# Linear attention's output side divided between both graph attentions (13 and 12 node tiles), and VectorE's copy of aggregated rows moved behind the next K copy

## The chip, the cores and the metric

The kernel runs on one core of a Trainium2 chip. Its time is the device time of one execution, in microseconds (us). The program writes instructions for five engines: TensorE (PE, with its weight loads shown as PEld), VectorE (DVE), ScalarE (ACT), GpSimd (POOL), and SyncE (SP), which mostly starts DMAs. Each engine works through its own queue in order; the queues meet only at semaphores.

## The reference, cut to what matters

There are 3125 nodes with 512 features and 53125 edges sorted by target. A layer of a mixed graph network is computed:

```
xn = layernorm(x)
# graph branch, two layers l = 0, 1
q, k, v = (xn @ Wq[l].T + bq[l]) / 8, xn @ Wk[l].T, xn @ Wv[l].T      # 8 heads of 64
w = softmax over the edges of one target of (q[dst] . k[src])
agg = segment_sum(w * v[src], dst);  attn = agg @ Wo[l].T + bo[l]
xn = batchnorm(xn + attn);  xn = batchnorm(xn + relu(xn @ W1.T + b1) @ W2.T + b2)
# mixing branch: linear attention on the first xn
q, k, v = softmax(xn Wq + bq), softmax(xn Wk + bk), xn Wv + bv         # softmax over a head's 64
mix = ((q @ (k.T v)) / (q . sum k) + q) @ Wp.T + bp
# then
x = x + layernorm(graph) + mix
out = x + mixture of 8 experts (top 2, 128 wide) on layernorm(x)
```

The change concerns the last line of the mixing branch, "mix", and the edge loop of the graph branch.

## The kernel before, in words

Stages follow one another: normalising and turning x; the Q, K and V products of layer 0 (stored in DRAM as Qd0 and KVd0); the mixing branch's products, which store the softmaxed q rows in DRAM (mixq) and leave the block matrix BD = k.T v in SBUF; the first graph attention; the joining of cut segments, the output product, batch norms and feed-forward of layer 0; the products of layer 1 (Qd1, KVd1); the second graph attention; the rest of layer 1; the experts.

**A graph attention** (`attend_pool`, `attend_pe`, `attend_dve`, `attend_act`) goes over 416 edge tiles of 128 edges. POOL gathers a tile's K and V rows with one indirect DMA (L1182, 128 rows of 4 KB) into a ring of 28 buffers. Eight tiles share one fetch of "slots", the rows of Q of the targets among them (L1191), and one indirect scatter of the aggregated rows (L1199). POOL may issue tile n once PE has turned tile n - 14, and once the buffer's former tile (n - 28) has been aggregated. The steps g = 0 to 105 each handle four tiles. In step g PE turns four K tiles (`turn_k`, L1270), runs the second half of an earlier group's aggregating matmuls after the second of them (`gather(..., 1)`, L1313), turns a one-hot tile for the slots in even steps (`turn_hot`, L1251) or the slots in odd ones (`turn_q`, L1262), turns the probabilities of group g - 2 (`turn_p`, L1277), adds masks (L1288), makes the scores (L1300), and runs the first half of the aggregation of group g - 2. Turned tiles go into PSUM banks that are used in a ring (`TURN_BANKS`: three banks in the first attention, five in the second). ACT copies three of four K tiles out of them (L1450) and makes the exponentials (L1469); DVE copies the fourth (`empty_k`, L1382), takes minima (L1375), normalises (L1389), copies turned probabilities (L1370), makes the one-hot tiles (L927), and copies the aggregated rows of eight tiles out of PSUM (`empty_agg`, L1395) for the scatter. `empty_agg` stands at the end of an odd step, ahead of the making of the one-hot tile.

**The mixing branch's output side** (`out_sp`, `out_pe`, `out_dve`, `out_act`) is written as generators that run in step with the first attention: every engine's loop calls `next(side)` at four places of a step. A node tile takes OUT = 16 such calls, so 25 tiles take 400 of the 424 calls. SP loads the tile's rows of mixq; PE turns them (L769, L770), multiplies with BD (L790, L792), turns the result again, and makes the product with Wp in twelve matmuls (L804 to L806: high and low parts of both factors); ACT and DVE copy and divide between; SP stores the rows to `mixd`, which the experts' stage reads. Wp is loaded once and cut into high and low parts during the first tile.

The second attention has no side work. Its K/V ring (`edge_views`) begins with buffers that are free early, and POOL issues nine gathers (`early`) before it waits for the stores of Q and for the end of the Q products. On SP's queue x is put away in DRAM (`put_x`, 6.25 MB) between the last K/V store and the first Q store of layer 1.

Of the kernel before, what the change touches and what calls it, by code (L numbers as in the profile page):

```python
# [6 lines left out]
P = 128  # L7
N, D, H, DH = 3125, 512, 8, 64
NT = 25
# [7 lines left out]
NJ = ET // NCH  # L17
# [65 lines left out]
def build(nc, A, out):  # L83
    with ExitStack() as ctx:
# [629 lines left out]
        TURN_BANKS, SC, AG = [[PS[4], PS[2], PS[3]], PS[0:5]], [PS[5], PS[6]], PS[7]  # L714
# [17 lines left out]
        OUT = 16  # L732
        WpH, WpL, WP_CUT = WoH, WA2r, 24
# [9 lines left out]
        def out_sp(views):  # L743
            qT, oT, qb, ob, outb, Wp = views
            sp.wait_ge(qkv_mm, QKV_E)
            sp.dma_start(Wp, kpo(A["MpT"])).then_inc(g_in, 16)
            sp.wait_ge(m_p, 3 * NT)
            sp.wait_ge(m_r, 3 * NT)
            sp.dma_start(rowsb[:, 1, :], A["mbp"].partition_broadcast(P)).then_inc(row_in, 16)
            for i in range(2):  # L750
                sp.wait_ge(mq_st[i], 16 * uses(NT, 2, i))
            fetch_q(0, qb)
            yield
            for s in range(OUT * NT):
                t, k = divmod(s, OUT)
                if k == 8 and t + 1 < NT:
                    fetch_q(t + 1, qb)
                if k == 15:
# [4 lines left out]
        def out_pe(views):  # L763
# [9 lines left out]
            pe.wait_ge(g_in, 16)  # L773
            pe.wait_ge(m_bd, 1)
            for s in range(OUT * NT):
                t, k = divmod(s, OUT)
                r = ROWS[t]
                if k == 0:
                    pe.wait_ge(mq_in, 16 * (t + 1))
                    if t:  # L780
                        pe.wait_ge(m_out, t)
                    features(PS[0], t, qb, m_qf)
                if k == 3:
                    pe.wait_ge(m_qe, t + 1)
                    if t == 0:
                        pe.wait_ge(*next_of(jd_seen))
                    if t:
                        pe.wait_ge(b_read, t)
                    for f in range(3):
                        pe.matmul(PS[0][0:r, 130 * f:130 * (f + 1)], qT[:, f, 0:r], BD[:, f, :], start=(f == 0),  # L790
                                  stop=(f == 2), skip_group_check=True)
                    pe.matmul(PS[1][0:r, 0:130], qT[:, 3, 0:r], BD[:, 3, :], start=True, stop=True,  # L792
                              skip_group_check=True).then_inc(m_c, 1)
                if k == 7:
                    pe.wait_ge(m_out, t + 1)
                    features(PS[1], t, ob, m_of)
                if k >= 10 and k < 14:
                    i = k - 10
                    if i == 0:
                        pe.wait_ge(m_oe, 2 * t + 2)  # L800
                    if t == 0:
                        pe.wait_ge(w_lo, WP_CUT + i + 1)
# [4 lines left out]
                    if k == 13:  # L807
                        mm.then_inc(m_b, 1)
                yield

        def out_dve(views):
# [3 lines left out]
            for s in range(OUT * NT):  # L815
                t, k = divmod(s, OUT)
                r = ROWS[t]
                di = small[0:r, 24:32]
                if k == 4:
# [15 lines left out]
                if t == 0 and k in (3, 5, 6, 7):  # L835
                    i = (3, 5, 6, 7).index(k)
                    dve.wait_ge(w_hi, WP_CUT + i + 1)
                    dve.tensor_tensor(WpL[:, i, :], Wp[:, i, :], WpH[:, i, :].bitcast(F32), ALU.subtract).then_inc(w_lo, 1)
                if k == 9:
# [3 lines left out]
                if k == 14:  # L843
# [6 lines left out]
        def out_act(views):  # L850
            qT, oT, qb, ob, outb, Wp = views
            yield
            for s in range(OUT * NT):
                t, k = divmod(s, OUT)
                r = ROWS[t]
                if k == 1:
# [4 lines left out]
                if k == 8:  # L861
# [4 lines left out]
                if t == 0 and 2 <= k < 6:  # L866
                    if k == 2:
                        act.wait_ge(g_in, 16)
                    act.activation(WpH[:, k - 2, :], Wp[:, k - 2, :], ACT.Copy).then_inc(w_hi, 1)
                yield  # L870

        def out_done(e):
            e.wait_ge(m_b, NT)
            e.wait_ge(b_read, NT)
# [293 lines left out]
        def attend_pool(l, begin):  # L1168
# [35 lines left out]
            early = (4, 9)[l]  # L1204
# [152 lines left out]
        def attend_dve(l, side, begin, work_free):  # L1357
# [372 lines left out]
        def stats_pe(l):  # L1730
            edges_done(pe, l)
            if l == 0:
                out_done(pe)
# [162 lines left out]
        WO_CUT = (28, 44)  # L1896
# [216 lines left out]
        sides = out_sp(views), out_pe(views), out_dve(views), out_act(views)  # L2113
# [12 lines left out]
        out_done(sp)  # L2126
# [7 lines left out]
        sp.wait_ge(m_st, 16 * NT)  # L2134
# [47 lines left out]
        def x_done(e):  # L2182
            if e == 2 * NT:
                is_normal(sp, 1, NCK - 1)
                put_x(1)

# [24 lines left out]
        ends_sp(1)  # L2211
        layer_weights(1)
# [25 lines left out]
        def cut_second(c):  # L2238
            if 2 <= c < 6:
                act.wait_ge(g_in, 16 + 16)  # L2240
# [545 lines left out]
```

## Time and profile before

| what | value |
|---|---|
| median of 3 runs | 3026.67 us (3017.48 to 3028.88) |
| the profiled execution | 3025.99 us, span 3024.7 us |
| PE, PEld busy | 2594.7 us (86%), 2114.9 us (70%) |
| DVE, ACT, POOL busy | 1647.1 (54%), 1327.2 (44%), 1129.9 us (37%) |
| DMA moved | 647.37 MB, of it 466.78 MB by POOL's indirect DMAs |
| first attention | about 527 to 1255 us of the span |
| second attention | about 1710 to 2378 us |

Busy time is the time in which an engine works on an instruction; idle time before an instruction is put down to what released it, an engine and a line. "issue" is a wait that the profile shows no releaser for. The chain is the row of work that ended last, followed back from the end. A granted clock of 1.00 means TensorE's full 2.4 GHz. The DMA share is the mean busy share of the 16 DMA engines.

### The profile page before, as it was taken

The page shows a single profiled execution, that of the slowest core. Times are in us where ns is not written, and L with a number is a line of the kernel's source. Part 1 is how long each engine was busy: PE and PEld are TensorE (multiplying, and loading weights), DVE is VectorE, ACT ScalarE, POOL GpSimd, SP SyncE. Part 2 cuts the span into 40 slices and gives each one's busy share as a digit, 9 for nine tenths or more (in the row PEclk, how much of TensorE's full clock was granted, in tenths as well). Part 3 has the DMA queues.
Part 4 walks back from the last instruction along what each step waited for, and adds up shares of the span by engine and source line. Part 5 has one row for each costly group of instructions (what it writes and reads, how often), then busy time and mean ns, then how long its engine had stood idle before and what let it go on. Part 6 is the DMA issues. An engine that isn't in the chain of part 4 may idle for free.

```text
span 3024.7 us, 78903 instructions
## 1 busy us (share of the span) xinstructions
PE 2594.7 (86%) x32457; PEld 2114.9 (70%) x32457; DVE 1647.1 (54%) x3354; ACT 1327.2 (44%) x3694; POOL 1129.9 (37%) x1128
## 2 busy tenths in 40 slices
PE   5989997999999999678897788888888679589998
PEld 4867885888787878456686677777777465477776
DVE  5226776666565666646412455555555646666653
ACT  3323443555555555422231365566555322334432
POOL 0000001777776767200001277777777211122110
PEclk8989998999999999889998899999999889699998
DMA  5662003999999999650125499999999731122211
GB/s 199 230 256 99 32 29 114 354 340 344 337 349 328 343 335 344 178 175 16 49 96 216 161 354 351 355 353 353 355 348 351 233 116 55 39 90 96 70 63 57
DMA packets 233911, 647.37 MB, mean 214 GB/s; under 512 B 39072, under 2 KB 45856, under 8 KB 231491
## 3 DMA queue, kind: packets, MB, share of 16 engines
q0 software_dynamic: 137088, 466.78, 42.4%
q1 hardware_dynamic: 96451, 175.38, 16.8%
q8 instruction: 263, 4.31, 0.6%
q14 instruction: 109, 0.89, 0.1%
HBM read 551.60 MB, written 116.19 MB: 221 GB/s over the span
## 4 chain that ended last, share of the span: by engine, by line
PE 66%; DMA 14%; DVE 9%; issue 6%; POOL 3%; ACT 2%; SPq 1%; DVEq 0%; POOLq 0%; ACTq 0%
PE ps L1270 9%; PE ps L1313 5%; PE ps L1300 5%; PE ps L595 4%; PE ps L596 4%; PE ps L597 4%; DMA Y<-KVd,srcE 4%; PE ps L1277 3%; PE ps L999 2%; PE ps L1001 2%; PE ps L1000 2%; DMA Qd<-stage 2%; PE ps L1953 2%; PE ps L1955 2%; PE ps L1954 2%
## 5 line engine op out<-in xcount | busy, mean ns | idle before, releaser
L1182 POOL DMA_INDIRECT Y<-KVd,srcE x360 | 341.9, 950 | 157.1 <-issue 68.6
L1469 ACT ACTIVATE stage<-ps,stage 128x128 f32<-128x128 f32 x832 | 294.8, 366 | 66.6 <-PE ps L1277 63.7
L1450 ACT ACTIVATE work<-ps 128x512 f32<-128x512 f32 x309 | 180.2, 597 | 296.7 <-PE ps L1270 296.4
L595 PE MATMUL ps<-Wh,xs 128*128 128x512 f32 x600 | 240.5, 401 | 55.9 <-DVE xs L535 55.9
L1370 DVE COPY G<-ps 128x512 f32<-128x512 f32 x208 | 143.8, 691 | 258.1 <-PE ps L1277 251.5
L1450 ACT ACTIVATE G<-ps 128x512 f32<-128x512 f32 x315 | 183.1, 597 | 218.5 <-PE ps L1270 217.7
L596 PE MATMUL ps<-Wl,xs 128*128 128x512 f32 x600 | 238.0, 397 | 0.0
L597 PE MATMUL ps<-Wh,xs 128*128 128x512 f32 x600 | 237.8, 396 | 0.0
L1182 POOL DMA_INDIRECT WA<-KVd,srcE x120 | 114.8, 957 | 321.2 <-PE ps L597 276.6
L1270 PE MATMUL ps<-ident,Y 128*128 128x128 f32 x1440 | 204.7, 281 | 33.1 <-DMA Y<-KVd,srcE 24.0
L1375 DVE TENSOR_REDUCE stage<-ps 128x4 f32<-128x512 f32 x208 | 143.8, 692 | 124.5 <-PE ps L1300 124.3
L1182 POOL DMA_INDIRECT xT<-KVd,srcE x188 | 179.3, 954 | 70.9 <-issue 33.2
L1270 PEld LDWEIGHTS ps<-ident,Y 128*128 128x128 f32 x1440 | 159.3, 142 | 59.4 <-issue 36.3
L535 DVE TENSOR_TENSOR xs<-xT,xs 128x512 fp32r<-128x512 f32 (+1 forms) x100 | 67.8, 679 | 231.9 <-ACT xs L560 231.9
L595 PEld LDWEIGHTS ps<-Wh,xs 128*128 128x128 f32 x600 | 113.9, 190 | 82.8 <-DVE xs L535 33.0
L1182 POOL DMA_INDIRECT mt<-KVd,srcE x45 | 43.9, 975 | 340.2 <-DMA KVd<-stage 315.2
L1469 ACT ACTIVATION_READ_ACCUMULATOR stage<-ps,stage 128x1 f32 x832 | 169.2, 203 | 0.0
L1313 PE MATMUL ps<-Y,G 128*32 128x64 f32 x5760 | 138.5, 221 | 11.9 <-issue 10.2
L1191 POOL DMA_INDIRECT stage<-Qd,segs x36 | 39.9, 1107 | 289.8 <-DVE segs L946 197.8
L1389 DVE TENSOR_TENSOR stage<-stage,st 128x512 f32<-128x512 f32 x208 | 144.0, 692 | 7.1
L571 ACT ACTIVATE stage<-ps 128x512 f32<-128x512 f32 (+1 forms) x100 | 59.6, 597 | 176.4 <-PE ps L597 176.4
L1277 PE MATMUL ps<-ident,stage 128*128 128x128 f32 x832 | 130.1, 279 | 7.3 <-issue 3.5
(403 smaller groups left out, 7071.8 us busy)
## 6 DMA issues: line engine op xcount, KB each, us to landing
KVd<-stage SPq DMA_DIRECT2D x96, 256.0 KB, 2.0
xTd<-xT SPq DMA_DIRECT2D x2, 6250.0 KB, 26.4
xT<-xTd SPq DMA_DIRECT2D x2, 6250.0 KB, 26.6
aggd<-work SPq DMA_DIRECT2D x6, 2048.0 KB, 7.4
Qd<-stage SPq DMA_DIRECT2D x48, 256.0 KB, 2.0
G<-aggd SPq DMA_DIRECT2D x48, 256.0 KB, 2.7
Y<-in_x SPq DMA_DIRECT2D x4, 1536.0 KB, 14.7
G<-mixq SPq DMA_DIRECT2D x24, 256.0 KB
```

What stands on the lines that cost most here:

```text
L595: pe.matmul(PS[e % 4][0:r, :], xh, Wh[:, w, k, :], start=(k == 0), stop=False)
L596: pe.matmul(PS[e % 4][0:r, :], xh, Wl[:, w, k, :], start=False, stop=False)
L597: mm = pe.matmul(PS[e % 4][0:r, :], xl, Wh[:, w, k, :], start=False, stop=(k == 3))
L1182: pool.indirect_dma_start(out=kvs[a], out_offset=None, in_=KVd[l][:, :], in_offset=bass.IndirectOffsetOnAxis(ap=srcE[:, n:n + 1], axis=0)) ...
L1270: mm = pe.transpose(bank[:, k * P:(k + 1) * P], kvs[a][:, k * P:(k + 1) * P], ident[:, :])
L1277: mm = pe.transpose(bank[:, i * P:(i + 1) * P], pT[g % len(pT)][:, i * P:(i + 1) * P], ident[:, :])
L1300: mm = pe.matmul(bank[32 * k:32 * k + 32, at], qblk[j % 2][:, k, 2 * (c % 4) + c // 4, :], kT[n % len(kT)][:, k * P:(k + 1) * P], start=Fa ...
L1313: mm = pe.matmul(AG[32 * i:32 * i + 32, DH * h:DH * (h + 1)], probs[x][:, i, h, :], kvs[a][:, D + DH * h:D + DH * (h + 1)], start=(x == 0 ...
L1370: dve.tensor_copy(probs[x][:, :, :, CAP * x:CAP * (x + 1)], bank[:, :].rearrange("p (c h s) -> p c h s", c=4, h=H)).then_inc(out_d, 1)
L1389: dve.tensor_tensor(p4, p4, rec4[:, :].unsqueeze(2).to_broadcast([P, 4, P]), ALU.mult).then_inc(normed, 1)
L1450: act.activation(kT[n % len(kT)], banks(l)[place_of(l, "k", n) % len(banks(l))][:, :], ACT.Copy).then_inc(out_a, 1)
L1469: last = act.activation(pT[g % len(pT)][:, P * i:P * (i + 1)], SC[g % 2][:, P * i:P * (i + 1)], ACT.Exp, bias=smin[:, t:t + 1], scale=-1.0 ...
```

## The change

The output side's generators take the layer: tiles 0 to 12 run beside the first attention and 13 to 24 beside the second, with OUT = 32 calls a tile, so that the tile's operations stand twice as far apart. Wp is loaded and cut a second time for the second attention: SP's load of it stands right behind `put_x(1)`, ahead of the Q stores. As the side uses banks PS[0] and PS[1] and some buffers, the second attention gets the first one's ring of three turn banks, six K buffers instead of seven, another order of K/V buffers, and `early` = 4. In both attentions `empty_agg` moves from the end of an odd step to the following step, behind DVE's K copy. The counts in waits on the shared semaphores follow.

```
             else:
-                kvs = [mt[:, 512 + 1024 * i:1536 + 1024 * i] for i in range(2)] + [pair(rowsb, 2)] + spare + kvs + [
-                    pair(G, i) for i in (0, 2, 10)] + [pair(rowsb, 0)] + moved[0:3]
-                kT += [G[:, 12 + i, :] for i in range(4)]
+                kvs = [mt[:, 512:1536], pair(rowsb, 2)] + spare[0:2] + kvs + [pair(G, i) for i in (0, 2)] + moved
+                kT += [G[:, 12 + i, :] for i in range(3)]
...
-        TURN_BANKS, SC, AG = [[PS[4], PS[2], PS[3]], PS[0:5]], [PS[5], PS[6]], PS[7]
+        TURN_BANKS, SC, AG = [[PS[4], PS[2], PS[3]] for l in range(2)], [PS[5], PS[6]], PS[7]
...
-        OUT = 16
-        WpH, WpL, WP_CUT = WoH, WA2r, 24
+        OUT = 32
+        WpH, WpL, WP_CUT = WoH, WA2r, (24, 44)
+        OUT_TILES = [range(0, 13), range(13, NT)]
+
+        def out_steps(l):
+            return itertools.product(OUT_TILES[l], range(OUT))
...
+        def out_weights():
+            sp.dma_start(WA[:, 2], kpo(A["MpT"])).then_inc(g_in, 16)
...
-                if k == 3:
+                if k == 6:
                     pe.wait_ge(m_qe, t + 1)
...
-                if k == 7:
+                if k == 14:
                     pe.wait_ge(m_out, t + 1)
                     features(PS[1], t, ob, m_of)
-                if k >= 10 and k < 14:
-                    i = k - 10
+                if k in (20, 22, 24, 26):
+                    i = (k - 20) // 2
...
-            early = (4, 9)[l]
+            early = 4
...
                 next(side, None)
                 if 4 * g + LOOK[l] + 1 < ET:
                     empty_k(4 * g + LOOK[l] + 1)
+                if g > AGG_AT and (g - 1 - AGG_AT) % 2:
+                    empty_agg((g - 1 - AGG_AT) // 2)
                 next(side, None)
...
                     normalise(g - 1)
-                if g >= AGG_AT and (g - AGG_AT) % 2:
-                    empty_agg((g - AGG_AT) // 2)
                 if x == 1 and b + 3 < NJ:
                     one_hot(l, b + 3)
                 next(side, None)
+            empty_agg(NJ - 1)
...
             if e == 2 * NT:
                 is_normal(sp, 1, NCK - 1)
                 put_x(1)
+                sp.wait_ge(w2_mm, WO)
+                out_weights()
...
+        views = out_views(G)
+        sides = out_sp(1, views), out_pe(1, views), out_dve(1, views), out_act(1, views)
+        for side in sides:
+            next(side)
         attend_pool(1, begin1)
-        attend_pe(1, iter(()))
-        attend_dve(1, iter(()), begin1, work_free1)
-        attend_act(1, iter(()), begin1, work_free1)
+        attend_pe(1, sides[1])
+        attend_dve(1, sides[2], begin1, work_free1)
+        attend_act(1, sides[3], begin1, work_free1)
```

## Rows read from the trace of the kernel before

**Rows 1.** Stretches: length, busy PE, PEld, DVE, ACT, POOL, clock, DMA share, GB/s
```profile
600.00:1200.00 600.00, 558.85 (x11191) 482.41 (x11184) 362.89 (x829) 339.73 (x1066) 426.50 (x428) 1.00 0.94 340
1760.00:2360.00 600.00, 507.02 (x11454) 435.16 (x11457) 318.53 (x606) 355.46 (x1121) 456.99 (x470) 0.98 0.96 353
1730.00:1740.00 10.00, 10.00 (x245) 8.85 (x241) 6.73 (x13) 7.08 (x25) 7.56 (x9) 1.00 1.00 389
1610.00:1640.00 30.00, 14.52 (x65) 11.70 (x63) 6.80 (x11) 3.79 (x6) 8.52 (x9) 0.80 1.00 394
```

**Rows 2.** Stretches, POOL's K/V gathers (L1182) alone: busy, count, clock, DMA
```profile
600.00:1200.00 600.00, 323.55 (x342) 1.00 0.94 340
1760.00:2360.00 600.00, 359.04 (x376) 0.98 0.96 353
```

**Rows 3.** The same for the slot fetches (L1191), first attention
```profile
600.00:1200.00 600.00, 51.23 (x43) 1.00 0.94 340
```

**Rows 4.** The same for the scatters (L1199), first attention
```profile
600.00:1200.00 600.00, 51.71 (x43) 1.00 0.94 340
```

**Rows 5.** Waits, POOL, 1760 to 2360: us in total, times, longest
```profile
POOL Y L1182 <- issue: 32.6, 107, 0.3
```

**Rows 6.** Waits, POOL, 600 to 1200
```profile
POOL Y L1182 <- PE ps L1313: 23.0, 17, 2.7
```

**Rows 7.** PE's groups, 600 to 1200: busy, mean ns, idle before
```profile
L1251 PE MATMUL ps<-ident,Y 128*128 128x128 f32 x42 | 12.7, 301 | 29.7 <-DVE G L1382 19.8 <-DVE work L1382 9.8
```

**Rows 8.** Chain in order of time, 1000 to 1030: start, length, what
```profile
1003.11 0.63 PE ps L1313 x32
...
1003.76 0.04 DVE xT L1395
...
1004.65 0.61 DVE G L1382
...
1005.40 0.30 PE ps L1251
...
1007.99 0.87 PE ps L790 x6
1008.86 0.22 PE ps L792 x2
...
1014.36 0.48 PE ps L769 x3
1014.84 0.11 PE ps L770
...
1019.12 0.23 PE ps L804
...
1025.23 0.23 PE ps L806
```

**Rows 9.** POOL in order of time: start, length, what, idle before
```profile
528.66 0.93 POOL L1182 DMA_INDIRECT mt<-KVd,srcE  x1 [4.88 <-PE ps L1270]
...
1226.96 0.94 POOL L1182 DMA_INDIRECT xT<-KVd,srcE  x1 [0.30 <-issue]
...
2358.44 0.93 POOL L1182 DMA_INDIRECT G<-KVd,srcE  x1 [0.30 <-issue]
```

**Rows 10.** Chain at the end of each attention
```profile
1254.29 0.70 DVE stage L1395
...
2377.32 0.70 DVE stage L1395
```

**Rows 11.** Chain and POOL's first early gather, ahead of the second attention
```profile
1611.61 26.89 DMA Qd<-stage
...
1617.74 1.00 POOL L1182 DMA_INDIRECT mt<-KVd,srcE  x1 [315.21 <-DMA KVd<-stage]
```

**Rows 12.** DMA issues: count, KB each, us to landing
```profile
G<-mixq SPq DMA_DIRECT2D x24, 256.0 KB
...
WA<-in_MpT SPq DMA_DIRECT2D x1, 1024.0 KB, 13.3
```

More of the change, by code:

```diff
@@ L741, in fetch_q, with out_sp @@
             sp.dma_start(qb[0:ROWS[t], :], mixq[P * t:P * t + ROWS[t], :]).then_inc(mq_in, 16)
-        def out_sp(views):
+        def out_weights():
+            sp.dma_start(WA[:, 2], kpo(A["MpT"])).then_inc(g_in, 16)
+        def out_sp(l, views):
             qT, oT, qb, ob, outb, Wp = views
[L745 to L752, printed above, removed]
+            if l == 0:
+                sp.wait_ge(qkv_mm, QKV_E)
+                out_weights()
+                sp.wait_ge(m_p, 3 * NT)
+                sp.wait_ge(m_r, 3 * NT)
+                sp.dma_start(rowsb[:, 1, :], A["mbp"].partition_broadcast(P)).then_inc(row_in, 16)
+                for i in range(2):
+                    sp.wait_ge(mq_st[i], 16 * uses(NT, 2, i))
+            else:
+                sp.wait_ge(qkv_mm, 2 * QKV_E)
+            fetch_q(OUT_TILES[l][0], qb)
             yield
-            for s in range(OUT * NT):
-                t, k = divmod(s, OUT)
-                if k == 8 and t + 1 < NT:
+            for t, k in out_steps(l):
+                if k == 16 and t + 1 in OUT_TILES[l]:
                     fetch_q(t + 1, qb)
-                if k == 15:
+                if k == 30:
                     sp.wait_ge(b_read, t + 1)
@@ L772, in out_pe @@
             yield
-            pe.wait_ge(g_in, 16)
+            pe.wait_ge(g_in, 16 * (l + 1))
             pe.wait_ge(m_bd, 1)
-            for s in range(OUT * NT):
-                t, k = divmod(s, OUT)
+            for t, k in out_steps(l):
                 r = ROWS[t]
@@ L814, in out_dve @@
             dve.wait_ge(row_in, 16 * 5)
-            for s in range(OUT * NT):
-                t, k = divmod(s, OUT)
+            for t, k in out_steps(l):
                 r = ROWS[t]
                 di = small[0:r, 24:32]
-                if k == 4:
+                if k == 8:
                     dve.wait_ge(m_c, t + 1)
@@ L834, in out_dve @@
                     dve.tensor_tensor(ob[0:r, :], ob[0:r, :], qb[0:r, :], ALU.add).then_inc(m_out, 1)
-                if t == 0 and k in (3, 5, 6, 7):
-                    i = (3, 5, 6, 7).index(k)
-                    dve.wait_ge(w_hi, WP_CUT + i + 1)
+                if t == OUT_TILES[l][0] and k in (6, 10, 12, 14):
+                    i = (6, 10, 12, 14).index(k)
+                    dve.wait_ge(w_hi, WP_CUT[l] + i + 1)
                     dve.tensor_tensor(WpL[:, i, :], Wp[:, i, :], WpH[:, i, :].bitcast(F32), ALU.subtract).then_inc(w_lo, 1)
-                if k == 9:
+                if k == 18:
                     dve.wait_ge(m_oe, 2 * t + 1)
@@ L848, in out_dve, with out_act @@
                 yield
-        def out_act(views):
+        def out_act(l, views):
             qT, oT, qb, ob, outb, Wp = views
             yield
-            for s in range(OUT * NT):
-                t, k = divmod(s, OUT)
+            for t, k in out_steps(l):
                 r = ROWS[t]
-                if k == 1:
+                if k == 2:
                     act.wait_ge(m_qf, t + 1)
@@ L865, in out_act, with out_done @@
                     act.activation(oT[0][:, :, 0:r], k4(PS[1][:, :])[:, :, 0:r], ACT.Copy).then_inc(m_oe, 1)
[L866 to L869, printed above, removed]
+                if t == OUT_TILES[l][0] and k in (4, 6, 8, 10):
+                    i = k // 2 - 2
+                    if i == 0:
+                        act.wait_ge(g_in, 16 * (l + 1))
+                    act.activation(WpH[:, i, :], Wp[:, i, :], ACT.Copy).then_inc(w_hi, 1)
                 yield
-        def out_done(e):
-            e.wait_ge(m_b, NT)
-            e.wait_ge(b_read, NT)
+        def out_done(e, l):
+            e.wait_ge(m_b, OUT_TILES[l][-1] + 1)
+            e.wait_ge(b_read, OUT_TILES[l][-1] + 1)
         ordb = ordE[:, :].rearrange("p (j x q) -> p j q x", x=2, q=4)
@@ L1895, in build @@
         WA_IN = [48 * (l + 2) for l in range(2)]
-        WO_CUT = (28, 44)
+        WO_CUT = (28, 48)
         def wo_high(l):
@@ L2112, in build @@
         views = out_views(G)
-        sides = out_sp(views), out_pe(views), out_dve(views), out_act(views)
+        sides = out_sp(0, views), out_pe(0, views), out_dve(0, views), out_act(0, views)
         for side in sides:
@@ L2125, in build @@
         ends_sp(0)
-        out_done(sp)
+        out_done(sp, 0)
         layer_weights(0)
@@ L2185, in x_done @@
                 put_x(1)
+                sp.wait_ge(w2_mm, WO)
+                out_weights()
         qkv_sp(1, x_done)
@@ L2205, in work_free1 @@
             e.wait_ge(w2_mm, WO)
+        views = out_views(G)
+        sides = out_sp(1, views), out_pe(1, views), out_dve(1, views), out_act(1, views)
+        for side in sides:
+            next(side)
         attend_pool(1, begin1)
-        attend_pe(1, iter(()))
-        attend_dve(1, iter(()), begin1, work_free1)
-        attend_act(1, iter(()), begin1, work_free1)
+        attend_pe(1, sides[1])
+        attend_dve(1, sides[2], begin1, work_free1)
+        attend_act(1, sides[3], begin1, work_free1)
+        for side in sides:
+            for _ in side:
+                pass
         ends_sp(1)
+        out_done(sp, 1)
         layer_weights(1)
```

21 lines of the change are left out of this document (10 added, 11 removed).

## The prediction

> **What bounds the kernel now.** I read the 40-slice picture of the page first: the reader is to see two long stretches, slices 7 to 16 and 22 to 31, where POOL goes from 0 to 7 tenths. They are the two graph attentions. Then I read both as stretches of 600 us from their middles [rows 1]. In the first PE is busy 558.85 of 600 us, in the second 507.02; the DMA engines show 0.94 and 0.96.
>
> What matters is who waits. I count in pairs: two groups of four edge tiles, for which POOL issues eight K/V gathers, one fetch of slots and one scatter. In the first attention 342 gathers pass in 600 us, in the second 376 [rows 2]: a pair takes 14.04 and 12.77 us. In the second, POOL's idle time before a gather is 0.30 us each time, put down to issue and never longer [rows 5]: POOL issues without a pause, and its issuing alone sets 12.77 us. In the first, POOL does wait, up to 2.7 us, for the gathering matmuls (L1313) to free a K/V buffer [rows 6]: there PE sets the pace. POOL's own pair in the first would be 8 x (323.55/342 + 0.30) + (51.23/43 + 0.30) + (51.71/43 + 0.30) = 9.97 + 1.49 + 1.50 = 12.96 us [rows 2 to 4].
>
> So the first attention is bound by PE at 14.0, with a floor under it of 12.96 from POOL; the second already lies on that floor.
>
> **The first attention's pair, from PE.** Two things go.
>
> (a) The moved copy. Today VectorE copies the aggregated rows at the end of an odd step and waits for matmuls that PE only runs in the next one. The chain shows it [rows 8]: the gathering matmuls end at 1003.74, DVE copies the rows (L1395), then makes the one-hot tile (L927, which stands between them), then copies K (L1382, to 1005.26), and only then the turn of the next hot tile (L1251) can start at 1005.40, because of a ring of three turn banks. PE's own idle time there is 29.7 us over 42 turns [rows 7], 0.70 us a pair. Behind the K copy, the copy of rows finds its matmuls done (PE runs them while DVE copies K), and neither the one-hot tile nor the K copy is behind a wait. I take the whole 0.70; the ends are 0 and 0.70. The scatter that waits for the copy gets it at most one K copy (0.7 us) later, with POOL some steps behind PE once POOL sets the pace: nothing.
>
> (b) Half of the side work. A tile costs PE two turns of features (0.48 + 0.11 each), the context products (0.87 + 0.22) and twelve output products, which start at 1019.12 and end at 1025.46 with other work between them; their own pieces on the chain sum to 3.2 us [rows 8]. Together 5.5 us. Now 16 steps make a tile and a pair takes 8, so half a tile, 2.7 us; with 32 steps a quarter, 1.4 us.
>
> PE's pair becomes 14.04 - 0.70 - 1.4 = 11.9 us, below POOL's 12.96. So what is late next is POOL, and the first attention should run at 12.96. Half the side work alone (12.7) would get there too; the moved copy alone would stop at 13.3.
>
> From the first gather that waited for PE (528.66) to the last (1226.96) are 698.3 us for 400 gathers [rows 9], 50 pairs of 14.0. At 12.96 that is 52 us less. The first three steps stay as slow as they are (weights are cut there, the ring is filling): 3 us given back, so -49. The tail shrinks too: from the last gather's end to the last copy's end there are 27.1 us in the first attention, where PE is behind with landed tiles, and 18.6 in the second [rows 9, 10]. That is 8 less, but the thirteenth tile's last matmuls now lie in this tail (step 410 of 424 instead of none beyond 400), 3 us: -5. First attention: -54 us.
>
> **The second attention.** On PE a quarter of a tile a pair is added, with three turn banks for five and six K buffers for seven. With these very sizes the first attention would need 11.9 us, so POOL's 12.77 hides both; were that cover gone, each 0.1 us a pair costs 5 us. DVE is busy 318.53 and ACT 355.46 of 600 us [rows 1]; a quarter tile adds under 1 us a pair to each. PE's new waits on the side (features copied, rows divided) have a group of matmuls between maker and user, as twice the steps lie between them; behind such a wait stand the next turns of K, for which POOL waits only 14 tiles later.
>
> What costs is POOL's order at the start. Nine gathers are issued before the wait for the Q table now, four after. The other five come behind it, in a queue that never pauses: 5 x 1.26 = +6.3 us. On the other side, these nine gathers run while x is being put away on SP's queue, and the first Q store waits 26.89 us behind that [rows 11]; the DMA engines are full there, 394 GB/s [rows 1]. Five gathers of 0.52 MB leave, and the second load of Wp (1.05 MB [rows 12]) joins SP's queue ahead of the Q stores: -1.57 MB, -4 us at that rate, as the Q products stall on this very store. If the gathers do not slow SP's queue, it is +2.7 instead; I take -4, as the engines are full. The loads of rows of q and stores of mixd, 0.131 MB a pair (one each of 256 KB a tile [rows 12]), use a queue that competes with the gathers: between 0 and +25 us (rival one); I take +3, since the engines have carried 389 GB/s in this attention [rows 1]. Four more copies on ACT and four on DVE are beside it: 0. The new load of mixq for tile 13 is issued while VectorE clears slots: 0, at most the few us of one load. Second attention: +6.3 - 4 + 3 = +5 us.
>
> **Sum.** -54 + 5 = -49. The profiled execution took 3025.99 us (span 3024.7), 0.68 below the median of the runs, 3026.67: 2977 us.
>
> The Trainium skill speaks against this at one place. In "SBUF — State Buffer", section "SBUF: two separate sides", HBM gives one NeuronCore about 358 GB/s. The second attention moves 353 x 12.77 = 4.51 MB a pair; with 0.131 more, an estimate from that page is 12.96 us instead of 12.77, which puts +10 in place of my +3: 2984. The row with 389 GB/s over 10 us disagrees with it as a hard limit.
>
> **Rivals.** *One: the DMA engines become the bound.* Share times pair is 0.94 x 14.04 = 13.20 us in the first attention and 0.96 x 12.77 = 12.26 in the second [rows 1, 2]; the difference, 0.94, is half a tile's transfers. With a quarter tile both need 12.73. If 0.96 is as high as the share goes for long, the pair is 13.26 in both: first -37 - 5, second +25 + 2, so -15: 3011. For it: the second attention sits at 0.96 throughout. Against: POOL explains that pace exactly, and shorter stretches read 1.00 [rows 1].
>
> *Two, slower than before: PE's queue is held in the second attention by the ring of three banks and the side's waits.* If these, rather than the work I counted, make the first attention's 14.04, then taking work out leaves it at 13.3 (only the gap of 0.70 goes) and the second rises from 12.77 to 14.04: 50 x (1.27 - 0.70) = +28, +2 at the start, and a tail as long as the first's, +8: 3064. It decides from a common pair of 13.4 us on: above it, what the second loses is more than what the first gains. For it: five banks are given up. Against: outside the 29.7 us, PE is idle only 11 us of the first attention's 600.
>
> *Three, faster still:* the first attention's slot fetches and scatters also shorten, its pair falls to the second's 12.77, and the late tile costs the tail nothing: 50 x 1.23 - 3 + 8 = 67, less the start's 2: 2961.
>
> *Four: the moved copy does nothing, as the turn of the hot tile waits for the K copy in any case.* Then PE's pair is 12.6, still below 12.96: no other time, and only the trace would tell. It shares the forecast's chance.
>
> **Chances and range.** Forecast 0.65 (its own range 2965 to 2995), rival one 0.19, rival two 0.07, rival three 0.09. A measurement of this kernel tells a change from none at about 0.5%, 15 us. Forecast and three are faster than that; rival one lies on the line, split 0.09 and 0.10 between faster and same; rival two is slower. Faster 0.83, same 0.10, slower 0.07. The range, 2950 to 3014, takes in rivals one and three, and leaves out two and the far ends of the others.
>
> **What would show it.** Right: POOL's idle time before gathers is 0.30 us in both attentions; 370 gathers in 600 us of the first; no idle time of PE before L1251 put down to VectorE; the last aggregated copy of the first attention near 1201; the second one's length from first slot fetch to last copy 5 to 10 us more. Wrong: POOL waiting for L1313 or L1270 in the second attention (rival two), or a DMA share of 0.96 with POOL waiting for PE and PE for DMA in both (rival one), or Q stores later than now behind x and Wp.

## The result, and the profile after

The changed kernel takes 3002.35 us (median of 4 runs, 2998.97 to 3005.04), the kernel before 3024.68 beside it: ratio 0.9928, 95% interval 0.9905 to 0.9951. It is faster, by 22 us where 49 were forecast. Measured once more beside each other (e12 below), the two stood at 3000.20 and 3023.57.

The profiled execution of the changed kernel took 2998.97 us, with a span of 2997.6; it is the fastest of its four, so its span lies 27 us under the kernel before's where the medians differ by 22. VectorE's code now has L1389 for the K copy, L1402 for the copy of aggregated rows; the gathers are L1189, the gathering matmuls L1320, the turn of the hot tile L1258.

The two attentions as stretches, in the columns of [rows 1]:

```profile
600.00:1150.00 550.00, 505.45 (x10719) 439.27 (x10718) 327.44 (x750) 323.06 (x1032) 414.12 (x426) 0.99 0.97 359
1700.00:2300.00 600.00, 540.91 (x11473) 463.06 (x11471) 337.78 (x672) 349.62 (x1116) 453.32 (x462) 0.99 0.97 356
```

The same for POOL's gathers alone, as [rows 2]:

```profile
600.00:1150.00 550.00, 325.22 (x342) 0.99 0.97 359
1700.00:2300.00 600.00, 355.82 (x370) 0.99 0.97 356
```

In the first attention 342 gathers now pass in 550 us instead of 600, so the pair fell to 12.9 us; in the second 370 pass in 600, where [rows 2] has 376: the second became slower. Where each attention begins and ends is read from POOL's gathers in order of time (the first, the 41st and the last of the second, and the last of the first):

```profile
1173.06 0.94 POOL L1189 DMA_INDIRECT xT<-KVd,srcE  x1 [0.30 <-issue]
...
1562.04 1.00 POOL L1189 DMA_INDIRECT mt<-KVd,srcE  x1 [314.75 <-DMA KVd<-stage]
...
1712.50 0.94 POOL L1189 DMA_INDIRECT Y<-KVd,srcE  x1 [0.31 <-issue]
...
2322.80 0.94 POOL L1189 DMA_INDIRECT xT<-KVd,srcE  x1 [0.30 <-issue]
```

and from the chain, as [rows 10, 11]:

```profile
1200.69 0.70 DVE stage L1402
...
1555.92 29.34 DMA Qd<-stage
...
2351.97 0.70 DVE stage L1402
```

The first attention's last copy ends at 1201.39 instead of 1254.99: -53.6. The second attention, from its first gather to its last copy, takes 2352.67 - 1562.04 = 790.6 us, and took 2378.02 - 1617.74 = 760.3 [rows 10, 11]: +30.3. The way between them and what follows give some 4 us. So the first attention came out as forecast, and the second gave more than half of it back. Six other traces below have the same first attention (e3, e4, e5, e6, e11, e12); there its last copy ends 2 to 8.5 us later, so -53.6 is the good end of what it does and some -50 the middle.

To see where, I cut each attention at the starts of its gathers: the first 40 (start), the next 352, which are 44 pairs, the last 23, and the tail from the start of the last gather to the end of the last copy. In the kernel before, the 41st gather of the second attention is this row of POOL's timeline:

```profile
1759.15 0.95 POOL L1182 DMA_INDIRECT Y<-KVd,srcE  x1 [0.30 <-PE ps L1270]
```

| second attention, us | before | changed | difference | forecast |
|---|---|---|---|---|
| start, 40 gathers | 141.4 | 150.5 | +9.1 | +6.3 - 4 |
| 44 pairs | 563.6 | 571.7 | +8.1 | +3 with the row below |
| last 23 gathers | 35.7 | 38.6 | +2.9 | |
| tail | 19.6 | 29.9 | +10.3 | 0 |

What PE waits for in both kernels is the clue. The changed kernel's waits of PE in 600 to 1150 and then 1700 to 2300 (us in total, times, longest):

```profile
PE ps L1320 <- issue: 24.6, 23, 2.2
PE ps L1258 <- DVE G L1389: 5.5, 5, 1.1
...
PE ps L1320 <- issue: 25.6, 25, 2.4
PE ps L1258 <- DVE G L1389: 6.3, 6, 1.1
...
PE ps L1277 <- DMA Y<-KVd,srcE: 5.1, 4, 2.9
...
PE ps L1277 <- DMA G<-KVd,srcE: 1.3, 1, 1.3
```

The kernel before, the same two stretches:

```profile
PE ps L1313 <- issue: 8.9, 14, 1.4
...
PE ps L1270 <- DMA Y<-KVd,srcE: 22.5, 33, 1.8
...
PE ps L1270 <- DMA WA<-KVd,srcE: 8.7, 16, 1.5
PE ps L1270 <- DMA mt<-KVd,srcE: 8.2, 11, 2.3
PE ps L1313 <- issue: 7.9, 9, 2.1
```

POOL's waits in 1700 to 2300 of the changed kernel now have some on the gathering matmuls that are longer than its usual 0.3 us:

```profile
POOL Y L1189 <- PE ps L1320: 5.4, 6, 1.6
...
POOL xT L1189 <- PE ps L1320: 2.8, 2, 2.5
```

Before, PE waits for gathered tiles to land in the second attention: it is ahead of POOL. Changed, it hardly does, and it stands three times as long inside the gathering matmuls, a loop without a semaphore wait. Such a pause is called a stand below. One in PE's timeline, after 25 of 32 matmuls:

```profile
2323.39 0.58 PE L1320 MATMUL ps<-xT,G 128*32 128x64 f32 x25
2326.01 0.32 PE L1320 MATMUL ps<-xT,G 128*32 128x64 f32 x7 [2.04 <-issue]
```

The trace lists DMA packets by queue, and one queue carries instructions, 16 KB a packet, 92 of them in 1700 to 2300 (90 before):

```profile
q8 instruction: 92, 1.51, 1.0%
```

PE runs 22,944 matmuls and weight loads in that stretch, some 250 for each of the 92 packets. Each of the 38 stands over 0.5 us inside L1320 in these two stretches ends 1.2 to 1.6 us after such a packet is done; so do all 14 of the kernel before. Of all matmuls of that line only one in ten starts so long after a packet. I read the stands as PE running out of instructions.

The stands come in bursts, and between them PE catches up. At each gather one can count the tiles that are issued and that PE has not yet turned. In the kernel before they are 10 to 13 in the first attention (14 is the most that POOL may be ahead) and some 4.5 in the second, never over 9, with 5 at its last gather. In the changed kernel's second attention they are 12 at its 115th gather, 3 at its 340th, and 12 at its last. PE's largest wait in a calm part, 2040 to 2220, and in the burst at the end, 2220 to 2340:

```profile
PE ps L1277 <- DMA Y<-KVd,srcE: 5.1, 4, 2.9
...
PE ps L1320 <- issue: 14.9, 10, 2.4
```

The calm part has no wait of L1320 at all. The places belong to PE's program: seven traces have the same first attention, and 100 of their 119 stands over 0.5 us lie at its tiles 170 to 215 and 345 to 395; four have the same second, and 68 of 76 lie at tiles 75 to 137 and 355 to 410. Why at these tiles is not shown.

### The profile page after: what moved, and what is told of

Read it like the earlier page. It is cut to its first block, busy times and chain, and to the rows that moved or that the text cites. A ratio compares the mean times of both kernels' runs of the same rounds, so it can differ in the third digit from the quotient of the medians.

```text
span 2997.6 us, 78921 instructions
## 1 busy us (share of the span) xinstructions
PE 2589.2 (86%) x32457; PEld 2113.5 (71%) x32457; DVE 1642.2 (55%) x3358; ACT 1318.9 (44%) x3698; POOL 1123.7 (37%) x1128
## 4 chain that ended last, share of the span: by engine, by line
PE 75%; DVE 9%; DMA 8%; issue 5%; ACT 2%; POOL 1%; SPq 0%; DVEq 0%; POOLq 0%; ACTq 0%
PE ps L1277 12%; PE ps L1307 7%; PE ps L1320 7%; PE ps L595 4%; PE ps L596 4%; PE ps L597 4%; PE ps L1284 4%; PE ps L1006 2%; PE ps L1008 2%; PE ps L1007 2%; DMA Qd<-stage 2%; PE ps L1960 2%; PE ps L1962 2%; PE ps L1961 2%; PE ps L1295 2%
## 5 line engine op out<-in xcount | busy, mean ns | idle before, releaser
L1189 POOL DMA_INDIRECT Y<-KVd,srcE x360 | 344.7, 958 | 141.8 <-issue 70.8
L1458 ACT ACTIVATE work<-ps 128x512 f32<-128x512 f32 x348 | 200.9, 597 | 334.5 <-PE ps L1277 334.3
L1189 POOL DMA_INDIRECT xT<-KVd,srcE x292 | 279.7, 958 | 92.7 <-issue 57.7
L1458 ACT ACTIVATE G<-ps 128x512 f32<-128x512 f32 x276 | 157.7, 595 | 169.1 <-PE ps L1277 169.0
L1277 PE MATMUL ps<-ident,Y 128*128 128x128 f32 x1440 | 198.7, 281 | 15.2 <-DMA Y<-KVd,srcE 8.0
L1189 POOL DMA_INDIRECT WA<-KVd,srcE x60 | 58.3, 972 | 297.5 <-PE ps L597 277.6
L1277 PE MATMUL ps<-ident,xT 128*128 128x128 f32 x1168 | 159.4, 278 | 3.9 <-issue 3.4
L1189 POOL DMA_INDIRECT mt<-KVd,srcE x30 | 29.4, 980 | 328.1 <-DMA KVd<-stage 314.7
L1320 PE MATMUL ps<-Y,G 128*32 128x64 f32 x5760 | 122.3, 221 | 25.6 <-issue 25.5
## 6 DMA issues: line engine op xcount, KB each, us to landing
xTd<-xT SPq DMA_DIRECT2D x2, 6250.0 KB, 25.8
```

Source lines behind the costliest of these rows:

```text
L1189: pool.indirect_dma_start(out=kvs[a], out_offset=None, in_=KVd[l][:, :], in_offset=bass.IndirectOffsetOnAxis(ap=srcE[:, n:n + 1], axis=0)) ...
L1277: mm = pe.transpose(bank[:, k * P:(k + 1) * P], kvs[a][:, k * P:(k + 1) * P], ident[:, :])
L1320: mm = pe.matmul(AG[32 * i:32 * i + 32, DH * h:DH * (h + 1)], probs[x][:, i, h, :], kvs[a][:, D + DH * h:D + DH * (h + 1)], start=(x == 0 ...
L1458: act.activation(kT[n % len(kT)], banks(l)[place_of(l, "k", n) % len(banks(l))][:, :], ACT.Copy).then_inc(out_a, 1)
```

## The experiments

Two theories. **S** (supply and slack): PE's work of 11.7 to 11.9 us a pair is what was forecast, but its stands for instructions and its short waits add some 1.1, so PE has no slack left under POOL's 12.8 to 12.9, taken over an attention. **Q or R**: the side costs the second attention by its own waits and order in the queues, or by the smaller ring and the fetch order. The table has, worked out from each trace as above, the pair (44 of them) and the tail of each attention, and of the second also the start and its whole length.

| kernel | median us | ratio, 95% interval | pair 1 | tail 1 | start 2 | pair 2 | tail 2 | second |
|---|---|---|---|---|---|---|---|---|
| before | 3024.68 | | 14.01 | 28.0 | 141.4 | 12.81 | 19.6 | 760.3 |
| changed | 3002.35 | 0.9928 [0.9905, 0.9951] | 12.91 | 28.3 | 150.5 | 12.99 | 29.9 | 790.6 |
| e1 copy alone | 2998.97 | 0.9925 [0.9908, 0.9941] | 13.49 | 26.3 | 141.4 | 12.83 | 20.7 | 761.9 |
| e2 split alone | 3046.81 | 1.0091 [1.0067, 1.0115] | 13.54 | 30.7 | 151.4 | 13.18 | 29.1 | 797.5 |
| e3 Wp early | 2996.60 | 0.9903 [0.9878, 0.9929] | 13.15 | 26.0 | 148.0 | 13.06 | 28.7 | 791.5 |
| e4 no side traffic | 2997.69 | 0.9915 [0.9898, 0.9933] | 12.93 | 27.6 | 150.5 | 12.97 | 27.6 | 786.0 |
| e5 half the gathered bytes | 2988.98 | 0.9890 [0.9871, 0.9909] | 13.00 | 27.9 | 150.8 | 13.02 | 15.6 | 775.2 |
| e6 side left out | 2986.99 | 0.9880 [0.9861, 0.9899] | 13.09 | 26.3 | 150.2 | 12.84 | 18.5 | 769.0 |
| e7 17 and 8 | 2997.31 | 0.9926 [0.9909, 0.9942] | 13.01 | 25.9 | 147.6 | 12.96 | 25.2 | 778.5 |
| e8 20 and 5 | 2998.23 | 0.9926 [0.9909, 0.9943] | 13.16 | 25.5 | 148.1 | 12.85 | 22.7 | 771.5 |
| e9 17 and 8, six early | 3001.39 | 0.9927 [0.9911, 0.9942] | 13.01 | 28.3 | 145.1 | 13.06 | 27.8 | 787.4 |
| e10 copy alone again | 2998.60 | 0.9921 [0.9908, 0.9934] | 13.39 | 26.5 | 141.0 | 12.83 | 20.0 | 761.3 |
| e11 one product of three | 2992.75 | 0.9898 [0.9882, 0.9913] | 13.01 | 27.9 | 150.2 | 13.24 | 18.8 | 787.2 |
| e12 changed again | 3000.20 | 0.9928 [0.9910, 0.9945] | 13.05 | 25.8 | 151.1 | 13.03 | 28.0 | 788.6 |

Single executions of kernels with a split spread over 6 to 27 us (e12: 2994.56 to 3009.4), and the stretch behind the second attention varies by 10 us between traces. The columns of one trace tell more than its total, but they vary too: the first attention that seven traces share has pairs of 12.91 to 13.15 and tails of 25.8 to 28.3, and a profiled execution can be an extreme one (e7's and e8's are the fastest of their six, e3's and e11's the slowest of their four, e4's and e6's the slowest of their six and five).

**e1, the moved copy alone**, all 25 tiles in the first attention.

```diff
-                if g >= AGG_AT and (g - AGG_AT) % 2:
-                    empty_agg((g - AGG_AT) // 2)
+                if g > AGG_AT and (g - 1 - AGG_AT) % 2:     # behind the next K copy
+                    empty_agg((g - 1 - AGG_AT) // 2)
```

> The kernel before with the moved copy alone (all 25 tiles still beside the first attention). Theory S (instruction supply): PE's queue is fed by blocks of instructions that DMA engines carry among the gathers' packets, and PE stands still inside a row of matmuls that have no wait between them when a block comes late; this grows as the DMA engines fill. The gap of 0.70 us a pair ahead of the hot tile's turn goes, but as the pair shortens the stalls inside the gathering matmuls rise from 9 to 15-25 us of 600, so the first attention's pair goes from 14.0 to about 13.6, -20 us: 3000 to 3010. Theory Q (the stall is the side work's own waits and does not depend on the DMA): the pair goes to 13.3, -35 us: about 2990. Both: the second attention is not changed by more than 3 us.

It takes as little time as the whole change. PE's turn of the hot tile no longer waits (first attention, as [rows 7]):

```profile
L1251 PE MATMUL ps<-ident,Y 128*128 128x128 f32 x41 | 11.2, 273 | 0.0
```

29.7 us of idle time are gone. The pair fell by 0.52 (0.62 in e10), not quite to the 13.3 that the prediction and Q gave for this half alone, and further than S's 13.6. The stands in the gathering matmuls rose from 8.9 to 11.2 us of 550, not to S's 15 to 25 of 600.

**e2, the split alone**: the changed kernel with the copy put back to the end of the odd step (the diff of e1, reversed).

> The changed kernel with the copy of aggregated rows put back where it was, so the split alone. The recorded forecast (PE's pair 12.6 us without the moved copy, still under POOL's 12.8 to 13.0): no other time than the changed kernel's, 3002 within 5. Theory S: PE's pair is about 13.0 in both attentions already, so 0.4 to 0.7 us a pair come back in each: +20 to +35 us in each attention, 3040 to 3070, so no gain over the kernel before and possibly a loss. Theory Q says the same as S here.

Slower than before. The same group in the first attention and in the second:

```profile
L1258 PE MATMUL ps<-ident,Y 128*128 128x128 f32 x41 | 12.6, 308 | 44.9 <-DVE G L1389 30.9 <-DVE work L1389 13.9
L1258 PE MATMUL ps<-ident,Y 128*128 128x128 f32 x45 | 14.1, 313 | 51.1 <-DVE G L1389 34.4 <-DVE work L1389 16.7
```

Half of the side work went, and the old wait grew from 29.7 us in 600 to 44.9 in 550. In the second attention, with its ring cut to three banks, the wait is there too. The prediction let "half the side work alone" reach POOL's floor; it stayed at 13.54. Against the changed kernel the first attention takes 28 us more, as expected; the second only 7, where 20 to 35 were expected.

**e3, the second load of Wp early**, before the second projections.

```diff
+            if e == 0:
+                sp.wait_ge(w2_mm, WO)
+                out_weights()
             if e == 2 * NT:
                 put_x(1)
-                sp.wait_ge(w2_mm, WO)
-                out_weights()
```

> The changed kernel with the second load of Wp ahead of layer 1's K/V stores on SP's queue, where the DMA engines are a quarter busy, and no longer between x's store and the first Q store. If Wp's 1.05 MB is what made the first Q store land 29.3 us after its issue instead of 26.9: the wait falls to 25 to 27 us and the time by 2.5 to 4 us (2998 to 3000). If SP's queue is held by x's own store at its own rate and Wp moved along beside it: no change.

The chain's Q store is back at its old length:

```profile
1562.11 26.84 DMA Qd<-stage
```

The start shortens from 150.5 to 148.0. The six other traces with the late load have 150.2 to 151.4, the two others with the early one 147.6 and 148.1. So the late load costs 2.5 us on that chain, and what is left of the start, 6.6, is about five gathers of 1.26. The median cannot show 2.5 us: the four executions lie between 2986.35 and 3013.25.

**e5, half the gathered bytes** in the second attention.

```diff
-  pool.indirect_dma_start(out=kvs[a], out_offset=None, in_=KVd[l][:, :],
+  to, rows = kvs[a], KVd[l][:, :]
+  if l == 1 and n >= KV:
+      to, rows = to[:, 0:D], Qd[l][:, :]
+  pool.indirect_dma_start(out=to, out_offset=None, in_=rows,
   ...
```

> The changed kernel with the second attention's gathers, from the 29th on, fetching rows of Q (2 KB) into the K half of the buffer and no V: the V half keeps older rows, so the second layer's attention is another one. Instructions of PE, DVE, ACT and their number are the same, POOL issues as many gathers, and the bytes of a gather are half. Theory S: the DMA share in the second attention falls from 0.97 to 0.5-0.6, the stalls of PE inside its gathering matmuls from 25 us of 600 to under 5, the backlog at the end goes, and the attention ends with a tail of 19 to 21 us instead of 30: -12 to -20 us against the changed kernel (2982 to 2990). Theory Q: PE's stalls stay above 20 us of 600 and the tail above 27; within 5 us of the changed kernel.

The stretch 1700 to 2300, and PE's waits in it:

```profile
1700.00:2300.00 600.00, 547.64 (x11717) 468.40 (x11716) 345.29 (x688) 358.78 (x1139) 459.49 (x462) 0.99 0.68 196
```

```profile
PE ps L1280 <- DMA Y<-Qd,srcE: 11.0, 8, 2.4
PE ps L1280 <- DMA xT<-Qd,srcE: 10.9, 14, 4.0
...
PE ps L1323 <- issue: 2.7, 5, 1.2
```

With the DMA engines at 0.68 the stands all but vanish, with PE's program and work as they were, and PE waits for tiles again, so it is ahead. (S expected a share of 0.5 to 0.6.) The two stands over 0.5 us that are left lie at tiles 104 and 112, inside the changed kernel's first burst. The tail falls from 29.9 to 15.6, with 3 tiles not yet turned at the last gather instead of 12. The pair does not fall: POOL now sets it alone, and its own instructions got longer (the mean of a gather, slot fetch or scatter is 0.998 us here, 0.982 in the changed kernel).

**e4, the side's transfers made tiny** in the second attention.

```diff
-  sp.dma_start(qb[0:ROWS[t], :], mixq[P * t:P * t + ROWS[t], :])
+  w = D if t < 14 else 16
+  sp.dma_start(qb[0:ROWS[t], 0:w], mixq[P * t:P * t + ROWS[t], 0:w])
   # the stores to mixd likewise, from tile 13 on
   ...   # the experts' stage reads rows of the first 13 tiles in place of these
```

> The changed kernel, but 11 of the second attention's 12 loads of a Q tile and all 12 stores of a finished tile carry 16 floats a row instead of 512 (23 transfers of 256 KB cut to 8 KB, some 5.7 MB of the second attention's 237 MB); those 12 tiles are wrong in the output. Instructions, waits and queues are unchanged. Theory S (PE stands because its next block of instructions comes late while the DMA engines are full): the stretch's share falls from 0.97 by some 0.02, PE's idle time inside the gathering matmuls falls from 25.6 us of 600 part of the way to the 9.7 that it had before, to 12 to 20, the pair from 12.96 to 12.80 to 12.90, and the median lies 3 to 10 us under the changed kernel's, 2992 to 2999. Theory Q (the side's own waits or its PE work cost the time, whatever the DMA engines do): idle time there stays at 24 to 27, the pair at 12.96, the median at 3000 to 3004.

```profile
1700.00:2300.00 600.00, 545.09 (x11562) 467.13 (x11551) 339.90 (x676) 352.78 (x1121) 456.12 (x464) 0.99 0.96 349
```

```profile
PE ps L1322 <- issue: 21.6, 18, 2.5
```

The share fell by 0.01, half of what I expected, the stands by 4 us, the second attention by 2.6 to 4.6 against the two traces of the changed kernel, which themselves differ by 2. The pair, 12.97, is Q's; the median, 2997.69, lies in S's range, but its interval overlaps the changed kernel's. So the side's own bytes are at most a small part.

**e6, the second attention's side left out**; ring, fetch order and late load stay. (The waits for the side's end and the experts' reads of its rows are adapted.)

```diff
-        attend_pe(1, sides[1])
-        attend_dve(1, sides[2], begin1, work_free1)
-        attend_act(1, sides[3], begin1, work_free1)
+        attend_pe(1, iter(()))
+        attend_dve(1, iter(()), begin1, work_free1)
+        attend_act(1, iter(()), begin1, work_free1)
 ...
```

> The changed kernel without any of the second attention's output side: its 12 tiles are not computed (wrong in the output), the second load of Wp, the ring that gave up buffers to the side and the fetch order with 4 early gathers stay. It prices those three alone. Theory S: without the side's PE work and its traffic the second attention's pair is back at 12.74 to 12.80, PE's idle time inside the gathering matmuls at 8 to 13 us of 600, the tail behind the last gather at 19 to 22 us, and of the extra 28 us only the 6.3 of the five later gathers and the 2.5 of the late Q store are left: 18 to 22 us under the changed kernel, 2978 to 2985, which is what the forecast of 2977 took the whole change to be. Theory R (the smaller ring and the four early gathers are the price): the pair stays at 12.9 or more and the median over 2993.

```profile
PE ps L1277 <- DMA Y<-KVd,srcE: 20.1, 22, 3.1
...
PE ps L1320 <- issue: 13.0, 16, 2.4
...
PE ps L1277 <- DMA xT<-KVd,srcE: 9.4, 16, 1.4
```

Pair and tail are those of the kernel before, PE waits for tiles again, and only the start keeps its +8.8. So of the 30 us, 9 are order and load; 21 come with the side: its work on PE, its transfers, and the stands, of which the second attention has 9 over 0.5 us here and 22 in the changed kernel. R is out for pair and tail as long as no side runs; whether the side would cost less with five turn banks, no run shows. The median lies 2 us above S's range.

**e7 and e8, 17 and 8 tiles, 20 and 5 tiles**, the load of Wp early in both.

```diff
-        OUT_TILES = [range(0, 13), range(13, NT)]
+        OUT_TILES = [range(0, 17), range(17, NT)]      # e8: 20
-        OUT = 32
+        OUT = (24, 48)                                 # e8: (20, 64)
 ...   # the places of a tile's operations among its steps follow; the load of Wp as in e3
```

> The changed kernel with 17 and 8 tiles in place of 13 and 12 (24 and 48 steps a tile), and the second load of Wp issued before the second projections, as in the run that loaded it early. Theory S: the first attention's pair 12.9 to 13.1 (PE's share of the side rises by four tiles, from 12.90), the second's between 12.85 and 12.93, its tail 25 us: 2990 to 2996. Theory R: the second attention's price is fixed (ring, early gathers, second load), so nothing comes back and the first pays for four tiles more: 3000 to 3008.

> As the kernel with 17 and 8 tiles, with 20 and 5 (20 and 64 steps a tile: the second attention's five tiles end 80 steps before its work does). Theory S: first pair 13.0 to 13.25, second 12.78 to 12.85 with a tail of 20 to 22 us, which is 8 us shorter: 2984 to 2994, the fastest of the three splits. Theory R: 3003 to 3012, worse than 17 and 8.

In these traces the second attention gives back what S said: 12 us at 17 and 8, 19 at 20 and 5, pair and tail near those of before. But both are of the fastest executions, 9 and 7 us under their medians, and both medians miss S's ranges. That the first attention pays is likely, as PE is busy 12.3 and 12.6 us of a pair there instead of 11.9, but the pairs, 13.01 and 13.16, do not show it: traces with 13 tiles reach 13.15. Both medians lie within 2 us of e1, which has no split. What I took for the best split does not exist; the medians are flat from 25 and 0 to 13 and 12.

**e9, as e7 with six gathers early**: two of G's buffers moved ahead in the ring.

```diff
-            early = 4
+            early = (4, 6)[l]
 ...
```

> The kernel with 17 and 8 tiles, with two of G's buffers put ahead in the second attention's ring so that 6 gathers go out before the tables are stored instead of 4 (the kernel before had 9, the changed one 4). If the five later gathers are what lengthened the way from the first gather of the second attention to the 41st (141.4 us before, 150.5 changed, 147.6 with 17 and 8), two gathers of 1.26 us come back: 144.5 to 146, and the median is 2 to 4 us under the 17 and 8 split's, some 2993 to 2996. If that stretch is longer for another reason (fewer buffers in the ring), it stays at 147 to 148 and the median with it.

The start did what it should:

```profile
1571.76 1.00 POOL L1190 DMA_INDIRECT mt<-KVd,srcE  x1 [315.12 <-DMA KVd<-stage]
...
1716.86 0.94 POOL L1190 DMA_INDIRECT Y<-KVd,srcE  x1 [0.30 <-PE ps L1278]
```

145.1 instead of 147.6, 1.25 a gather. The median missed: it is 4 us over e7's, with intervals that are the same. This trace has a longer pair and tail than e7's, but it is of a middling execution and e7's of the fastest, so that the edit caused it is not shown.

**e10 and e12, the copy alone and the changed kernel again**, on one chip.

> The kernel before with the copy of the aggregated rows moved and nothing else (all 25 tiles in the first attention), once more, to stand beside the changed kernel on one chip: 2996 to 3000, 2 to 5 us under the changed kernel, if dividing the side is worth nothing or less; over the changed kernel if the two earlier jobs differed by their chips.

> The changed kernel once more, for the other three to stand beside on one chip: 3000 to 3004.

2998.6 and 3000.2, with overlapping spreads: dividing the side gains nothing that shows on top of the moved copy.

**e11, a third of the side's products** in the second attention.

```diff
   mm = pe.matmul(PS[1][0:r, :], hi, WpH[:, i, :], start=(i == 0), stop=(l == 1 and i == 3))
+  if l == 0:                       # the two cross terms
       pe.matmul(PS[1][0:r, :], hi, WpL[:, i, :], start=False, stop=False)
       mm = pe.matmul(PS[1][0:r, :], lo, WpH[:, i, :], start=False, stop=(i == 3))
```

> The changed kernel with 4 of the 12 product matmuls of a tile in the second attention (the two cross terms with the low halves are left out, so those 12 tiles come out less exact). DMA traffic, ring, fetch order, the copies on VectorE and ScalarE and all waits stay; PE does 17.0 and 17.0 us less in 600, 0.74 us a pair. Theory L (PE's 11.7 us a pair and some 1.1 in which it waits for instructions leave no slack under POOL's 12.9, so PE ends the stretch behind and works off a full ring): with 0.74 of slack the pair is 12.84 to 12.92, the tail behind the last gather 19 to 23 us in place of 29.9, and the median 2986 to 2993. Theory Q (the side's order and waits in the queues cost it, whatever PE's work is): tail 27 to 30, pair 12.95 to 13.0, median 2999 to 3004.

L is S with its slack put in numbers. The median, 2992.75, is L's, and the tail, 18.8, just under its range; the pair, 13.24, is neither's. The profiled execution was the slowest of four (3004.27; two of the others took under 2990), and PE stood longer in it than anywhere:

```profile
PE ps L1321 <- issue: 33.2, 23, 2.6
PE ps L1278 <- issue: 10.5, 11, 1.9
```

Its 21 stands over 0.5 us inside L1321 end 1.2 to 1.6 us after an instruction packet as well. But the shorter program has moved them: the first row is of 1920 to 2200, the second of 2220 to 2340, where the changed kernel has 14.9 us.

```profile
PE ps L1321 <- issue: 31.8, 21, 2.6
...
PE ps L1321 <- issue: 1.4, 2, 0.9
```

The tiles not yet turned rise to 13 at the 215th gather, where the pair pays, and are 5 again at the last, and so the tail is short. So this trace does not show that less PE work shortens the tail: no burst lies at the end. The median lies 7 us under e12's, with intervals that just touch, so the smaller work probably does save time. What sets the number of stands is open: the DMA share alone does not, as e1 has 0.97 in its first attention and 11.2 us of them in 550, the changed kernel 0.97 and 24.6.

## Why the prediction was wrong

**The step that failed** is the one on the second attention: "With these very sizes the first attention would need 11.9 us, so POOL's 12.77 hides both". PE's work was sized nearly right: busy 505.45 of 550 us at 12.91 a pair is 11.9 in the first attention, and 540.91 of 600 at 12.99 is 11.7 in the second, where the 11.9 of the sum is 11.7 of work and 0.2 to 0.3 of idle time. Its idle time was not. The prediction let it fall to 11 us in 600 once the waits for VectorE were gone; the changed kernel has 45 in 550 and 59 in 600, of which waits for landed tiles are 2 and 7. The rest is 1.0 and 1.1 us a pair, most of it stands for instructions (24.6 and 25.6) and waits for VectorE that were to be gone (8.7 and 10.1). So over an attention PE needs 12.8 to 12.9, as much as POOL, and not 11.9, and the slack of 0.9 that was to hide the side was used up. It was not gone everywhere: between the bursts PE caught up from 12 tiles to 3. But the last burst lies before the end, and the tail pays for it.

- *First attention, -54:* measured -53.6. The pair is 12.91 where 12.96 was worked out, and that is partly luck: POOL's own pair fell to 12.80, as its slot fetches and scatters last 1.06 us each instead of 1.19 and 1.20 [rows 3, 4] (the first step of rival three), and waits for PE add 0.1. Inside the sum two small terms failed and cancelled: the tail kept its 28.3 us (-5 forecast), and the start was 3.8 shorter, where the first three steps were to stay slow (3 us given back).
- *The moved copy, 0.70 a pair:* 0.52 and 0.62 alone. Rival four, that it does nothing, is refuted by e1; it alone is worth the whole gain. *Half the side alone, 12.7:* 13.54, as the wait for VectorE grew when the work around it went.
- *Early gathers, +6.3:* right, 1.25 each (e9), 6.6 with Wp early.
- *Put-away and Q store, -4:* wrong sign, +2.5. The other end was named (+2.7, if the gathers do not slow SP's queue), and that is what happened: with four gathers and no load of Wp (e3) the store takes 26.84 us, with nine 26.89 [rows 11].
- *The side's transfers, +3:* e4 has 2.6 to 4.6 less, hardly more than two traces of one kernel differ. Rival one took a share of 0.96 for the limit; the share is 0.97, with POOL at its floor or 0.1 above it, so it named the right resource and the wrong place. *PE's side, 0:* +21 with those transfers (790.6 less e6's 769.0). About half is the tail, where PE works off the tiles of the last burst; the rest is POOL waiting for L1320 (five waits over 0.4 us in 1700 to 2300, 5.9 us beyond the usual 0.3; not one behind the start of this attention before [rows 5]) and its instructions, which last 0.982 us instead of 0.975 in the mean.
- *Rival two* named the right attention and the wait that would show it, POOL for the gathering matmuls, and priced it too high: a pair of 13.0, under its point of 13.4. Of its reason, the ring and the side's waits, PE's waits for VectorE before L1258 show a part (10.1 of 59 us); the stands are the larger part. Without the moved copy (e2) it came true in its sign: slower by 0.9%.

The sum: -53.6, +9.1 for +2.3 at the start, +11.0 for +3 to the last gather, +10.3 for 0 in the tail, -4 elsewhere, so -27 in span for -49, and -22 between the medians.

## What to carry to other kernels

Work moved under another engine's pace is free only if the idle time of the engine that receives it is slack; split that idle time into waits for data and the rest, and count the rest as work. An engine that hardly waits for its input any more has no slack over the whole stretch. Then look along the stretch at how far it is behind: the mean hides bursts, and a burst near the end comes out as a longer tail. Where two edits are made together, price each alone: here one was the whole gain, and the other only moved time from one stage to the next.

## What was not expected of the hardware

One DMA queue brings instructions in 16 KB packets, one each 6.5 us in these stretches; I take them to be TensorE's, as its stands end just behind them. Inside loops without any wait TensorE stood up to 2.4 us at a time, 24.6 us of 550 and 25.6 of 600 with the DMA engines 0.97 busy, and 2.7 of 600 at 0.68 with the same program. Most stands come at the same tiles in every trace of one program, and they move when the program changes. The Trainium skill, "Runtime: NRT & Kernel Launch", section "Instruction fetch mechanics", describes refills in 16 KiB blocks by a queue of their own, mostly hidden; the packets agree with that, and at 0.97 the hiding does not.
